# Chebyshev attention on one core: tiles taken batch by batch, the carried row added on VectorE from PSUM

## The reference

```python
xn = layernorm(x)
s = window_attention(xn)              # 16 heads of 8, window 64, rotary positions
g = silu(xn @ ternary(w).T * alpha + bias)
x = x + s * g

xn = layernorm(x)
q, k, v = split(xn @ W_in)            # second layer: Chebyshev attention
Tq, Tk = cheb(clip(q / sqrt(8))), cheb(clip(k / sqrt(8)))
kv = cumsum(Tk * v, axis=token)       # prefix sums along the sequence, per order
ks = cumsum(Tk.sum(-1), axis=token)
s = ((Tq * kv * beta).sum(order) / ((Tq.sum(-1) * ks * beta).sum(order) + 1e-7)) @ W_out.T
g = silu(layernorm(moe(xn) + xn))     # 8 experts, top 2, hidden width 512, GELU
x = x + s * g
```

## Time and profile before

| what | value |
|---|---|
| times of the runs shown | 858.42, 859.27, 861.26 us; median 859.27 |
| span of the profiled execution | 874.6 us |
| instructions | 22303 |
| PE busy | 596.5 us, 68% of the span |
| VectorE busy | 660.3 us, 75% |
| ScalarE busy | 441.9 us, 51% |
| GpSimd busy | 436.9 us, 50% |
| stages in the profiled execution | first layer to about 400 us; entry of the Chebyshev loop to 460; expert passes to 720; tail of the loop to 792; combining to the end |

### The profile page before, as it was taken

The page is one execution under the profiler, slowest core; times in us unless marked ns, Lnnn a source line. Parts: engine busy times, 40 slices in busy tenths (PEclk is TensorE's granted clock), DMA queues, the critical chain, the costliest instruction groups (busy, mean ns, idle before and its releaser), DMA issues.

```text
span 874.6 us, 22303 instructions
## 1 busy us (share of the span) xinstructions
PE 596.5 (68%) x7049; PEld 402.2 (46%) x7049; DVE 660.3 (75%) x1711; ACT 441.9 (51%) x1075; POOL 436.9 (50%) x697
## 2 busy tenths in 40 slices
PE   1898899998988988842327777777777775324220
PEld 0566666665655655520214555555555553112110
DVE  4688888888787677743845898899898898617777
ACT  1456555554544454410417787888888774101111
POOL 3145555555457677657703344444444343764721
PEclk9999999998999799965658999999999997555555
DMA  9999999200000000001121232323232321111211
GB/s 228 345 283 287 286 288 287 75 0 0 0 8 18 15 18 18 16 13 45 48 76 38 85 99 93 102 81 104 85 100 85 96 69 41 52 45 36 66 31 36
DMA packets 127372, 80.93 MB, mean 93 GB/s; under 512 B 11832, under 2 KB 118208, under 8 KB 127296
## 3 DMA queue, kind: packets, MB, share of 16 engines
q1 hardware_dynamic: 122160, 70.97, 27.2%
q0 software_dynamic: 5136, 9.02, 3.8%
HBM read 18.85 MB, written 49.55 MB: 78 GB/s over the span
## 4 chain that ended last, share of the span: by engine, by line
PE 34%; DVE 33%; issue 17%; POOL 7%; ACT 4%; SPq 1%; DVEq 1%; DMA 1%; another core or an unknown queue 1%; POOLq 0%; ACTq 0%
PE m_ps L1047 5%; PE e_ps L1059 4%; DVE yts L1394 3%; POOL experts_sb L563 3%; DVE mneg L1142 3%; PE y_ps L1010 2%; PE q_ps L954 2%; PE m_ps L823 2%; PE p_ps L1003 2%; DVE pr L1391 2%; PE y_ps L887 2%; DVE pr L1393 2%; ACT pexp L610 2%; DVE rot L1184 2%; PE m_ps L837 2%
## 5 line engine op out<-in xcount | busy, mean ns | idle before, releaser
L610 ACT ACTIVATE pexp<-e_ps 128x512 f32<-128x512 f32 x128 | 76.5, 598 | 75.4 <-PE e_ps L870 66.7
L1142 DVE TENSOR_REDUCE mneg<-m_ps 128x4 bf16<-128x512 f32 x128 | 84.7, 683 | 22.5 <-PE m_ps L837 22.2
L1047 PE MATMUL m_ps<-xs,wb 128*128 128x512 f16 x276 | 80.4, 403 | 19.8 <-issue 18.6
L563 POOL DMA_INDIRECT experts_sb<-ybuf,slots x64 | 63.5, 993 | 32.3 <-issue 18.9
L492 POOL DMA_INDIRECT xbuf<-x,slots x64 | 65.2, 1019 | 16.6 <-issue 14.9
L1019 PE MATMUL p_ps<-eye_sb,yn 128*128 128x128 f32 x32 | 11.6, 363 | 80.4 <-DVE yn L1399 64.2
L887 PE MATMUL y_ps<-pexp,vd 128*32 128x128 f32 x512 | 57.6, 295 | 3.1 <-ACT pexp L610 1.0
L557 POOL TENSOR_TENSOR pexp<-rot,pexp 128x512 f16<-128x512 f32 x24 | 27.8, 1157 | 56.6 <-ACT pexp L731 56.6
L851 PE MATMUL e_ps<-early 128*128 128x256 bf16 x256 | 52.0, 284 | 0.1
L557 POOL TENSOR_TENSOR pexp<-qt,pexp 128x512 f16<-128x512 f32 x24 | 30.3, 1264 | 43.1 <-ACT pexp L731 43.1
L1101 PE MATMUL e_ps<-b_sb,cwt 8*128 8x128 f32 x64 | 16.6, 436 | 49.3 <-ACT cwt L780 49.3
(11 more groups left out here) (223 smaller groups left out, 2129.7 us busy)
## 6 DMA issues: line engine op xcount, KB each, us to landing
xbuf<-zero_sb SPq DMA_DIRECT2D x71, 256.0 KB, 4.0
ybuf<-zero_sb SPq DMA_DIRECT2D x71, 256.0 KB, 3.6
wb<-experts_sb SPq DMA_DIRECT2D x46, 256.0 KB, 2.3
xs<-xbuf SPq DMA_DIRECT2D x23, 256.0 KB, 2.7
ybuf<-vd SPq DMA_DIRECT2D x23, 256.0 KB, 2.2
experts_sb<-in_experts_w SPq DMA_DIRECT2D x8, 512.0 KB, 6.9
x_all<-in_x SPq DMA_DIRECT2D x8, 256.0 KB, 5.3
xbuf<-x,slots POOLq DMA_INDIRECT x64
```

Source lines behind the costliest of these rows:

```text
L563: nc.gpsimd.indirect_dma_start(yg[:, 2 * (B * n + b) + k, :], None, ybuf, bass.IndirectOffsetOnAxis(ap=slots[:, k, B * n + b:B * n + b + 1 ...
L610: nc.scalar.activation(pexp[:, j, :, :], e_ps[j % 2][:, :, :], ACT.Exp, scale=float(D) ** -0.5).then_inc(exp_ready.sem, 1)
L1047: last = nc.tensor.matmul(u_ps[f % 2], wb1[:, i % 2, f, a, :], xg16[:, i % 2, b, :], start=k == 0, stop=k == len(PARTS) - 1)
L1142: nc.vector.tensor_reduce(mneg[:, n.batch, j // 2, (j % 2) * NG:(j % 2) * NG + NG], m_ps[j % 2][:, :, :], AX.X, ALU.max, negate=True).then ...
```

## The change

The loop takes the tiles batch by batch: `chebyshev_tile(c)` gives the place in memory of the c-th tile, c // 8 is its batch, and the carry comes from the tile just before, c - 1, with none for tiles 0, 8, 16 and 24. The tokens within each tile are permuted (on the host, with the rotary table, the masks and the triangular matrix to match) so that the last token of a tile lies on partition 96 instead of 127, which VectorE can read directly. `carry_on(c)` adds that row from PSUM onto row 0 of `kv`: two instructions, 1 partition by 432 and by 288 columns, one operand in SBUF and one in PSUM. It stands after `clip` and before `cheb_out`. ScalarE's `last_copy`, SP's `carry_row`, and the 720-column add in `cheb_keys` are gone, with their semaphores; PE's `sums(c)` waits for `carry_on(c)` instead of the copies.

```diff
-CHEB1, CHEB2 = 7, 8
+CHEB1, CHEB2 = 6, 8
+def chebyshev_tile(c):
+    return B * (c % TAUS) + c // TAUS
+def carries(c):
+    return c - c // TAUS
...
-            for c in range(LEAD - 1):
-                carry_row(c)
             weights_split.wait(sp, Tile(TAUS - 1, 3))
...
-                if c < NT - B:
-                    carry_row(c)
...
-                last_copy(c - 1)
...
-                pe.wait_ge(xn1_stored.sem, 4 * (c + 1))
-                nc.tensor.matmul(p_ps[:, 0:3 * C], xn1t_all[:, c, :], w_in[:, :], start=True, stop=True).then_inc(s_projected2, 1)
+                pe.wait_ge(xn1_stored.sem, 4 * (chebyshev_tile(c) + 1))
+                nc.tensor.matmul(p_ps[:, 0:3 * C], xn1t_all[:, chebyshev_tile(c), :], w_in[:, :], start=True, stop=True).then_inc(s_projected2, 1)
...
-                after(pe, s_carry_copied, min(c, NT - B))
+                after(pe, s_carried, 2 * carries(c))
...
-                if c >= B:
-                    dve.wait_ge(s_carry[c % B], 16 * (c // B))
-                    done(nc.vector.tensor_tensor(kv[0:1, c % 2, :], kv[0:1, c % 2, :], carry[0:1, c % B, :], ALU.add), False)
...
+            def carry_on(c):
+                dve.wait_ge(s_summed, c)
+                dve.wait_ge(s_keys, keys_steps(c + 1) - 1)
+                for k, (lo, hi) in enumerate(((0, 3 * SW), (3 * SW, 5 * SW))):
+                    nc.vector.tensor_tensor(kv[0:1, c % 2, lo:hi], kv[0:1, c % 2, lo:hi], cc_ps[k][LAST:LAST + 1, 0:hi - lo], ALU.add).then_inc(s_carried, 1)
...
                 if c + 2 < NT:
                     clip(c + 2)
+                if (c + 1) % TAUS:
+                    carry_on(c + 1)
                 cheb_out(c)
```

More of the change, by code:

```diff
@@ L46 @@
 LEAD = 4
+LAST = 96
 GROUPS = [(0, 14), (14, 28), (28, 32)]
@@ L105, in keys_steps @@
 def keys_steps(c):
-    return CHEB1 * c - min(c, B)
+    return CHEB1 * c
+def chebyshev_tile(c):
+    return B * (c % TAUS) + c // TAUS
+def carries(c):
+    return c - c // TAUS
 def after(engine, sem, value):
@@ L241, in program @@
         tb_ps = t_ps[:, :, :].rearrange("p a b -> p (a b)").bitcast(BF16)
-        carry = early[0:1, 0:B * ORD * SW].rearrange("p (b w) -> p b w", b=B)
-        last_sb = early[:, 0:2 * ORD * SW].rearrange("p (b w) -> p b w", b=2)
         y2, e2, res0, acc0 = (xs[:, i, :, :, :].rearrange("p h s d -> p (h s d)").bitcast(F32).rearrange("p (b c) -> p b c", b=B)
@@ L272, in program @@
         ybuf = nc.dram_tensor("ybuf", (BLOCKS * SLOT, C), F32, kind="Internal").ap()
-        s_carry = [sem(f"s_carry{b}") for b in range(B)]
         s_out = [sem(f"s_out{i}") for i in range(2)]
@@ L365, in program @@
         s_y_copied = sem("s_y_copied")
-        s_carry_copied = sem("s_carry_copied")
         s_oc_copied = sem("s_oc_copied")
@@ L373, in program @@
         s_outs = sem("s_outs")
+        s_carried = sem("s_carried")
         s_biased = sem("s_biased")
@@ L430, in load_rows @@
                 sp.dma_start(xin[:, i % 2, :, :], xbuf[bass.ds(place * SLOT, SLOT), :].rearrange("(k p) c -> p k c", p=P)).then_inc(s_rows_in[i % 2], 16)
-            def carry_row(c):
-                sp.wait_ge(s_carry_copied, c + 1)
-                sp.dma_start(carry[0:1, c % B, :], last_sb[P - 1:P, c % 2, :]).then_inc(s_carry[c % B], 16)
             def store(i):
@@ L696, in polynomials @@
                 nc.scalar.activation(t[:, 1, :, 0:C], poly[:, 0, :, :], ACT.Identity, scale=2 * R2 / C3, bias=shift[:, 0:1]).then_inc(s_poly, 1)
[L698 to L707, removed]
             def oc_copy(c):
@@ L717, in s1_copy @@
                 act.wait_ge(s_projected_out, c + 1)
-                nc.scalar.mul(s1_all[:, c, :], o_ps, 0.5).then_inc(s_s1_copied, 1)
+                nc.scalar.mul(s1_all[:, chebyshev_tile(c), :], o_ps, 0.5).then_inc(s_s1_copied, 1)
             def gelus(i, f):
@@ L1370, in cheb_keys @@
                 done(nc.vector.tensor_tensor(sums[:, :, 0:C], t[:, :, 1, 0:C], vs[:, c % 2, :].unsqueeze(1).to_broadcast([P, ORD, C]), ALU.mult), False)
-                done(nc.vector.tensor_reduce(sums[:, :, C:SW], t[:, :, 1, 0:C].rearrange("p j (h d) -> p j h d", d=D), AX.X, ALU.add), c >= B)
-                if c >= B:
-                    dve.wait_ge(s_carry[c % B], 16 * (c // B))
-                    done(nc.vector.tensor_tensor(kv[0:1, c % 2, :], kv[0:1, c % 2, :], carry[0:1, c % B, :], ALU.add), False)
+                done(nc.vector.tensor_reduce(sums[:, :, C:SW], t[:, :, 1, 0:C].rearrange("p j (h d) -> p j h d", d=D), AX.X, ALU.add), False)
                 done(nc.vector.tensor_reduce(t[:, :, 0, C:SW], t[:, :, 0, 0:C].rearrange("p j (h d) -> p j h d", d=D), AX.X, ALU.add), False)
                 assert at[0] == keys_steps(c + 1)
+            def carry_on(c):
[3 more added lines that the diff above has]
+                    nc.vector.tensor_tensor(kv[0:1, c % 2, lo:hi], kv[0:1, c % 2, lo:hi], cc_ps[k][LAST:LAST + 1, 0:hi - lo], ALU.add).then_inc(s_carried, 1)
             def cheb_out(c):
@@ L1464, in _, with place_of, places @@
             gate(TAUS - 1)
+def place_of():
+    at = np.arange(W)
+    at[[32, W - 1]] = at[[W - 1, 32]]
+    return at
+def places():
+    return (np.arange(T).reshape(-1, W)[:, place_of()]).reshape(-1)
 def constants():
     import numpy as np
+    at = place_of()
+    inside = places()[:P]
     inv = (1.0 / np.float32(10000.0) ** (np.arange(0, D, 2, dtype=np.float32) / np.float32(D))).astype(np.float32)
@@ L1472, in constants @@
     cos, sin = np.cos(ang), np.sin(ang)
-    rope = np.concatenate([cos, cos, sin, -sin], 1).astype(np.float32).reshape(TAUS, P, 2 * D).transpose(1, 0, 2)
-    q, k = np.arange(W)[:, None], np.arange(W)[None, :]
+    rope = np.concatenate([cos, cos, sin, -sin], 1)[places()].astype(np.float32).reshape(TAUS, P, 2 * D).transpose(1, 0, 2)
+    q, k = at[:, None], at[None, :]
     before, own = np.where(k >= q, 0, NEG), np.where(k <= q, 0, NEG)
@@ L1486, in constants @@
             "win_exp": win_exp.astype(f), "pair_sel": sel.astype(f),
-            "tri": np.triu(np.ones((P, P), f)), "descend": np.tile(np.arange(E, 0, -1).astype(f), (P, 1)),
+            "tri": (inside[:, None] <= inside[None, :]).astype(f), "descend": np.tile(np.arange(E, 0, -1).astype(f), (P, 1)),
             "earlier": np.triu(np.ones((P, P), f), 1), "slot_tab": np.tile(tab.astype(f), (P, 1))}
@@ L1513 @@
     arrays = {
-        "x": np.asarray(L0_attn_x),
+        "x": np.asarray(L0_attn_x)[:, places()],
         "proj_w": np.concatenate([w_attn[0:2 * C], w_attn[2 * C:3 * C][order]]).T,
@@ L1537 @@
     program(nc, **args)
-    return run_bass_kernel_spmd(nc, [given], core_ids=[0]).results[0]["out_0"]
+    return run_bass_kernel_spmd(nc, [given], core_ids=[0]).results[0]["out_0"][:, places()]
```

## The result

The changed kernel took 850.98 us (median of 848.83 to 854.01, four executions), the kernel before 858.9 beside it: a ratio of 0.9919, interval 0.9895 to 0.9943. A longer series later gave 853.16 (849.9 to 857.39, ten executions) against 857.3, ratio 0.9951, interval 0.993 to 0.9973. So the gain is between 4 and 8 us; the forecast was 8.3, the time 851.0, and the range 845.5 to 857.0.

What follows compares the result with a forecast made beforehand. Bounds: SP's queue delaying rows at the entry, ScalarE and PE in the passes, GpSimd's gathers at the end. Terms -9.3 + 0 + 1.0 = -8.3 us took 859.27 to 851.0 us, range 845.5 to 857.

Steps and rivals of the forecast that it cites:

- The entry: Tiles 0 to 2, before pass 0: rows ready before `yn`, first up-matmul at 450.9 instead of 460.21, gain 9.3 us.
- The pair in the entry: Before pass 0: three pairs of adds, 0.99 us each, delay the end of output step 2.
- The passes: The 23 expert passes: `yn` delayed 0.5 us under a cover of 0.8, so no gain and no loss.
- the GpSimd stall: VectorE's output step in a pass: standing still for GpSimd's subtraction, 0.88 us, passes from the 144-column to the 288-column add.
- The cover of 0.3 us: In a pass: what remains of VectorE's 0.8 us to spare when the pair delays `yn` by 0.5.
- both rivals: In the passes: thin cover, +9.5 us, time 860.5, chance 0.12; falling PE clock, +25 us, time 876, chance 0.06.
- or the GpSimd stall moves with it: Thin-cover rival, passes: the stall moves with the pair, each of 19 passes loses time, 860.5 us; chance 0.12.
- The tail: After the last pass's first half: copy, store and first gather move by one pair, 1.0 us lost.
- Loss 1.0: At the end: no GpSimd instruction absorbs the pair, so copy, store and first gather come 0.99 us later.
- the rival on PE's clock: In the passes: longer PE wait brings 15 more clock falls of 1.65 us, +25 us, time 876; chance 0.06.
- The sum: Whole kernel: entry -9.3, passes 0, end +1.0, together -8.3 us, from 859.27 to 851.0.
- The sign: Whole kernel: faster, meaning below 856.7 us, chance 0.82; within 0.3% 0.09; slower 0.09.

Runs made afterwards that it cites:

- e2: Against after: SP waits for the first two multiplies of tile 2's output step ahead of the expert loads; 860.28 us, ratio to before 1.0027.
- e4: Against after: the pair of adds and PE's wait for it left out, so the carry is missing; 845.1 us, ratio 0.9858.
- before: The kernel without the change; 858.9 us in the first series, 857.3 in the longer one; profiled twice.
- e3: Against after: every pair of adds issued twice, first into a row nobody reads; 898.42 us, ratio 1.0447.
- after: The changed kernel, against before; 850.98 us, ratio 0.9919, and in a longer series 853.16 us, ratio 0.9951; profiled twice.
- e8: Against after: the pair of adds behind the output step in iterations 0 to 2 only; 848.3 us, ratio 0.987.
- e6: Against after: the pair of adds behind the output step instead of ahead of it; 849.45 us, ratio 0.9911.
- e10: Against after: a dead copy of the pair's first add for tiles 1 to 3 only; 849.93 us, ratio 0.9912.

## Why the prediction was right, and where it was not

- **The entry: right.** Predicted gain 9.3 us; 9.8 against the profile it was made on, 8.2 against the second one, whose entry was 1.5 us shorter. Rows stood ready before `yn`, and `yn` ended the wait; putting the wait back (e2) costs 9.7 us of the entry. Loads issued at 408 to 414 and rows at 433, against 413 to 422 and 439.
- **The pair in the entry: right,** 3.2 us for three against 2.97 (e4).
- **The passes: right,** +0.2 or -0.8 us against the two profiles of before, where 0 was said, and by the mechanism named: the clip's wait took up the old add, the GpSimd stall went over to the 288-column add, and PE waits longer for `yn` and less for the rows. The rounds from the third on are 10.72 and 12.37 as before, but for the one of 12.97. The cover of 0.3 us held in all but that one, though it is thin: e3 shows both rivals from one more pair on. What the working lacked is that the stall can move on to a later step of the output: to `dn` in e3, and to `yn` in that round of after. The rival's "or the GpSimd stall moves with it" was the right worry.
- **The tail: the term was too small.** "Loss 1.0" is right for the pair itself (0.97, e8 against e6 and e4), and GpSimd's gathers are the limit behind it, as said. But in the profiles of after the tail lost 4.3 to 5.1 us against the first profile of before: besides the pair 2.7 for a long fall of PE's clock and 0.6 to 1.4 for the late store. The step that failed is the rival on PE's clock: it counted falls in the passes, where their number stayed, at 1.65 us each, and did not ask where they come to lie once the entry is 9 us shorter.
- **The sum.** By the traces it is -9.8 + 0.2 + 5.1 = -4.5 us against the first profile of before, -8.2 - 0.8 + 6.7 = -2.3 against the second, and the longer series says -4.1. The first series, -7.9, agrees with the predicted -8.3 more closely than the terms deserve: that closeness is luck. Both profiled executions of after (854.01 and 854.37) are slower than the medians of their series, so the tail of a typical execution may be shorter. Executions of after between 848.83 and 850.33 all show a mean granted clock of 0.861, the others 0.854 to 0.861; whether the late fall is missing in those was not traced.
- **The sign and the range held** in both series, with the median near the middle of the range in the first and in its slower half in the second.

## What to carry to other kernels

Look first at what stands ahead of the late transfer in its queue: here moving three lines behind the loads gave 845.79 us, more than rewriting the carry did, because it removes the wait and adds nothing to the path. A step that just fits under a cover of 0.3 us costs nothing, and its double costs 45 us, so the cover is a number to know before adding to it. And when an edit shifts a whole stretch of work, ask where the clock's falls will lie afterwards: the same work behind the last pass took 25.0 us in after and 22.3 in e10, by its place against them.

## What the hardware showed that was not expected

- With 1.1 us added to the entry the tail was 3.2 to 4.0 us shorter (26.75 against 29.98 and 30.79), and the whole not longer (849.93 against 850.98 and 853.16): PE ran at a granted clock of 1.00 in place of 0.50, 2.4 in place of 1.2 GHz, in the 5 us from 705 to 710.
- From the fourth round on, falls in the passes stood about 34 or 44 us apart, three or four rounds (once 24, in e2), in every kernel but e3, where most were one round apart, 13.7 us, and PE waited 3.59 us in most rounds.
- A VectorE instruction with a single SBUF input of 16 columns stood still until GpSimd was done, like one with two (1.11 in place of 0.17).
- An add on one partition, from PSUM partition 96 to SBUF partition 0, takes 0.60 and 0.45 us for 432 and 288 columns, as much as the multiplies on 128 partitions beside it.
- A store of 256 KB that took 2.2 us to land in the other traces took 3.6 and 2.8 us in the two where a packet of an instruction queue moved during it.
